# Attention states in 32-row tiles, and the output of four heads to a PSUM bank

## What is computed

```python
q = jax.nn.elu(q * E ** (-0.5)) + EPS_FEAT
k = jax.nn.elu(k) + EPS_FEAT
def step(carry, qkv_t):                       # one token after the other
    kv_s, k_s = carry
    q_t, k_t, v_t = qkv_t
    kv_s = kv_s + jnp.einsum('bhe,bhf->bhef', k_t, v_t)
    k_s = k_s + k_t
    num = jnp.einsum('bhe,bhef->bhf', q_t, kv_s)
    den = jnp.einsum('bhe,bhe->bh', q_t, k_s)[..., None] + EPS_DEN
    return ((kv_s, k_s), num / den)
...
return out @ W_out + b_out
```

## Time and profile before

| | us |
|---|---|
| median of 3 runs | 613.49 |
| lowest and highest | 611.41 to 614.47 |
| profiled execution, time | 610.65 |
| its span, first to last instruction | 608.9 |
| TensorE busy | 444.8 |
| VectorE busy | 345.6 |
| ScalarE busy | 237.6 |
| GpSimd busy | 331.3 |
| attention stage, about | 236 to 387 |

### The profile page before, as it was taken

One profiled execution on the slowest core, in us unless ns is written; L12 is line 12 of the kernel. 1 busy time (PEld: TensorE's weight loads), 2 busy tenths in 40 slices (PEclk: granted clock), 3 DMA queues, 4 the chain that ended last, 5 costly groups with the idle time before them and its releaser, 6 DMA issues.

```text
span 608.9 us, 12872 instructions
## 1 busy us (share of the span) xinstructions
PE 444.8 (73%) x4788; PEld 297.6 (49%) x4788; DVE 345.6 (57%) x984; ACT 237.6 (39%) x629; POOL 331.3 (54%) x259
## 2 busy tenths in 40 slices
PE   1884966997699325899999979149867599857970
PEld 1742543553345213677777768148335355433440
DVE  6396971221115992687777865485999222212097
ACT  4971212332224277555555530187611133322420
POOL 6184776888786601222222220004987788887691
PEclk9987875555569657799999986656978555555995
DMA  8998600101009980001111110541000000100592
GB/s 267 375 250 323 232 9 9 9 5 10 7 5 377 408 317 0 2 3 39 36 34 35 34 36 10 156 177 57 2 0 9 8 8 6 10 6 6 174 409 107
DMA packets 34389, 60.40 MB, mean 99 GB/s; under 512 B 12611, under 2 KB 18846, under 8 KB 33870
## 3 DMA queue, kind: packets, MB, share of 16 engines
q1 hardware_dynamic: 23078, 58.41, 26.8%
q0 software_dynamic: 11264, 1.38, 2.6%
HBM read 37.43 MB, written 29.36 MB: 110 GB/s over the span
## 4 chain that ended last, share of the span: by engine, by line
DVE 29%; PE 29%; issue 15%; DMA 13%; ACT 7%; POOL 5%; SPq 1%; POOLq 0%; DVEq 0%; another core or an unknown queue 0%; ACTq 0%
DVE X L973 9%; DMA rows_d<-A 5%; PE bank L897 5%; PE bank L778 4%; PE bank L878 4%; PE bank L795 3%; POOL planes_d L438 3%; DVE Cb L1075 3%; ACT A L508 3%; DMA planes_d<-Bb,put_i 2%; POOL A L452 2%; DVE bn L978 2%; DMA Bb<-planes_d 2%; PE bank L768 2%; PE bank L788 2%
## 5 line engine op out<-in xcount | busy, mean ns | idle before, releaser
L438 POOL DMA_INDIRECT planes_d<-Bb,put_i x64 | 100.4, 1569 | 24.6 <-issue 18.4
L452 POOL DMA_INDIRECT A<-rows_d,tok_i x64 | 71.9, 1124 | 20.6 <-issue 16.6
L1105 DVE TENSOR_TENSOR ring<-ring,bank 128x88 f32<-128x88 f32 x64 | 15.7, 246 | 103.7 <-ACT ring L576 72.0
L675 PE MATMUL bank<-ident,A 128*128 128x128 f32 x96 | 22.5, 412 | 55.1 <-ACT A L508 40.9
L479 POOL TENSOR_TENSOR Bb<-Cb,chm 128x576 f32<-128x576 f32 x16 | 19.0, 1220 | 66.8 <-DVE Cb L1139 33.4
L768 PE MATMUL bank<-ident,A 128*128 128x128 f32 x64 | 30.0, 469 | 29.3 <-DMA A<-rows_d,tok_i 23.2
L396 POOL TENSOR_TENSOR Bb<-Eb,st 128x512 f32<-128x512 f32 x8 | 8.9, 1112 | 74.7 <-DVE st L1023 74.7
L570 ACT ACTIVATE ring<-bank 128x128 f32<-128x128 f32 x64 | 17.7, 277 | 81.4 <-PE bank L768 70.7
L675 PEld LDWEIGHTS bank<-ident,A 128*128 128x128 f32 x96 | 18.2, 220 | 58.1 <-issue 29.9
L479 POOL TENSOR_TENSOR Bb<-w3s,chm 128x576 f32<-128x576 f32 x16 | 17.8, 1147 | 49.8 <-PE bank L920 49.8
L795 PE MATMUL bank<-w2s,ring 88*64 88x128 f32 x256 | 43.9, 446 | 0.0
(11 more groups left out here) (155 smaller groups left out, 1121.6 us busy)
## 6 DMA issues: line engine op xcount, KB each, us to landing
planes_d<-zeros SPq DMA_DIRECT2D x8, 2048.0 KB, 20.6
w3s<-in_w3T SPq DMA_DIRECT2D x2, 2816.0 KB
rows_d<-A SPq DMA_DIRECT2D x8, 512.0 KB, 11.5
A<-planes_d SPq DMA_DIRECT2D x8, 512.0 KB, 9.2
PL<-planes_d SPq DMA_DIRECT2D x8, 512.0 KB, 10.1
Cb<-planes_d SPq DMA_DIRECT2D x8, 512.0 KB, 10.8
Bb<-planes_d SPq DMA_DIRECT2D x8, 512.0 KB, 12.0
w1s<-in_w1T SPq DMA_DIRECT2D x1, 2816.0 KB
```

The costliest lines, as they stand in the source:

```text
L438: pool.indirect_dma_start(out=planes_d[f], in_=Y[:, s, :], in_offset=None, out_offset=bass.IndirectOffsetOnAxis(ap=put_i[:, s:s + 1], axis=0),
L452: pool.indirect_dma_start(out=A[:, t, :], out_offset=None, in_=rows_d, in_offset=bass.IndirectOffsetOnAxis(ap=tok_i[:, t:t + 1], axis=0), ...
L675: ins = pe.transpose(bank[g % 2][:, (i % 4) * P:(i % 4 + 1) * P], A[:, i, :], ident[:, :])
```

## The change

States. For each block q and chunk c, the 128x144 matmul becomes four of 128x32 rows and columns in the array: group j takes rows 32j to 32j + 31 of K's features (four heads) and the GW = 36 columns of those four heads, and its output goes to partitions 32j to 32j + 31 of one bank. A block's four chunks fit one bank (144 columns), so there are four batches (one per q) for eight, and `AFTER` is changed to suit. VectorE's mask is now `hm`, which says for each partition which of the four heads of its group it belongs to. SW holds 36 columns for each state where it held 144.

Output. The output goes to four banks, four heads each. The matmuls on the states take 32 partitions of QT and of SW, and 36 columns: 60 for 30. The four upper banks become one tensor, `upper`, so that the division runs once over all four banks.

Loop. TensorE's steps 1 to 6 are written out; the other engines keep their loops. The waits of the four engines that count `kv_ps` and `kv_sb` count four per step where they counted eight.

```diff
-    AFTER = ((), (0, 1, 2), (3, 4), (5, 6, 7))
+    AFTER = ((), (0, 1), (2,), (3,))
...
-        bank = [ctx.enter_context(nc.psum_tensor(f"bank{k}", [P, 512], F32)) for k in range(8)]
+        bank = [ctx.enter_context(nc.psum_tensor(f"bank{k}", [P, 512], F32)) for k in range(4)]
+        upper = ctx.enter_context(nc.psum_tensor("upper", [P, 4, 512], F32))
+        bank += [upper[:, k, :] for k in range(4)]
...
-                    for m in AFTER[g]:
-                        q = m // 2
-                        if m >= len(STATES):
-                            pe.wait_ge(kv_sb, PRIMED + NH * b + m + 1 - len(STATES))
-                        for k in range(1 if m == NH - 1 else 2):
-                            ins = pe.matmul(bank[STATES[m % len(STATES)]][:, k * VW:(k + 1) * VW], KN[:, 2 * (m % 2) + k, q, :],
-                                            VN[par][:, q, :, :].rearrange("p h f -> p (h f)"), start=True, stop=True)
+                    for q in AFTER[g]:
+                        if q >= len(STATES):
+                            pe.wait_ge(kv_sb, PRIMED + NQ * b + q + 1 - len(STATES))
+                        for c in range(NC if q < NQ - 1 else NC - 1):
+                            for j in range(4):
+                                ins = pe.matmul(bank[STATES[q % len(STATES)]][32 * j:32 * j + 32, c * GW:(c + 1) * GW],
+                                                KN[:, c, q, 32 * j:32 * j + 32],
+                                                VN[par][:, q, 4 * j:4 * j + 4, :].rearrange("p h f -> p (h f)"),
+                                                start=True, stop=True)
...
-                    ob = bank[4 + h // 8][:, 0:NC * HV].rearrange("p (c h f) -> p c h f", c=NC, h=8)
+                    ob = bank[4 + h // 4][:, 0:NC * GW].rearrange("p (c h f) -> p c h f", c=NC, h=4)
...
-                            before_c = SW[:, q, c - 1, :] if c else SW[:, q - 1, NC - 1, :]
-                            ins = pe.matmul(bank[4 + half][32 * q:32 * q + 32, c * HV:(c + 1) * HV], QT[par][:, t0:t0 + CHUNK],
-                                            before_c[:, half * HV:(half + 1) * HV], start=False, stop=True, skip_group_check=True)
+                            before_c = SW[rows, q, c - 1, :] if c else SW[rows, q - 1, NC - 1, :]
+                            o = c * GW
+                            ins = pe.matmul(bank[4 + g][32 * q:32 * q + 32, o:o + GW], QT[par][rows, t0:t0 + CHUNK],
+                                            before_c, start=False, stop=True, skip_group_check=True)
...
-            with pe.Fori(0, (B - 2) // 2) as i:
-                step(2 * i + 1, 1)
-                step(2 * i + 2, 0)
-            step(B - 1, 1, last=True)
+            for b in range(1, B):
+                step(b, b % 2, last=b == B - 1)
...
-                        dve.tensor_tensor(SW[:, q, 2 * (m % 2):2 * (m % 2) + n, :],
-                                          bank[STATES[m % len(STATES)]][:, 0:n * VW].rearrange("p (c v) -> p c v", c=n),
-                                          own[:, :].unsqueeze(1).broadcast_to([P, n, VW]), ALU.mult).then_inc(kv_sb, 1)
+                        dve.tensor_tensor(SW[:, q, 0:n, :].rearrange("p c (j f) -> p c j f", j=4),
+                                          bank[STATES[q % len(STATES)]][:, 0:n * GW].rearrange("p (c j f) -> p c j f", c=n, j=4),
+                                          hm[:, :].unsqueeze(1).unsqueeze(3).broadcast_to([P, n, 4, E + 1]),
+                                          ALU.mult).then_inc(kv_sb, 1)
...
-                for k in range(2):
...
+                dve.tensor_scalar(den.rearrange("p (g n) -> p g n", g=4), ob[:, :, :, E], DEN_EPS, None, ALU.add).then_inc(o_step, 1)
+                dve.wait_ge(o_step, 2 * b + 1)
+                dve.reciprocal(rec, den).then_inc(o_step, 1)
+                dve.wait_ge(o_step, 2 * b + 2)
+                dve.tensor_tensor(AN[:, :, :].rearrange("p c (g h f) -> p g c h f", g=4, h=4),
+                                  upper[:, :, 0:NC * GW].rearrange("p g (c h f) -> p g c h f", c=NC, h=4)[:, :, :, :, 0:E],
+                                  rec.rearrange("p (g c h) -> p g c h", g=4, c=NC).unsqueeze(4)
+                                  .broadcast_to([P, 4, NC, 4, E]), ALU.mult).then_inc(an_ready, 1)
```

More of the change, by code:

```diff
@@ L54, in macaron_kernel @@
     HV = VW // 2
+    GW = 4 * (E + 1)
     NQ = L // P
@@ L165, in macaron_kernel @@
         HTB, KT, QT0 = (Bb[:, o + k * L:o + (k + 1) * L] for k in range(3))
-        SW = Cb[:, 0:NQ * NC * VW].rearrange("p (q c v) -> p q c v", q=NQ, c=NC)
+        SW = Cb[:, 0:NQ * NC * GW].rearrange("p (q c v) -> p q c v", q=NQ, c=NC)
         VN0 = Cb[:, o:o + NQ * VW]
@@ L626, in copy_kn @@
                 act.wait_ge(kn_ps, b + 1)
-                act.wait_ge(kv_ps, PRIMED + NH * b)
+                act.wait_ge(kv_ps, PRIMED + NQ * b)
                 for c in range(NC):
@@ L828, in project @@
                 if not (isinstance(b, int) and b == 0):
-                    pe.wait_ge(kv_sb, PRIMED + NH * (b - 1))
+                    pe.wait_ge(kv_sb, PRIMED + NQ * (b - 1))
                     pe.wait_ge(q_read, 2 * b)
@@ L851, in turn_out @@
                     pe.wait_ge(kn_sb, PRIMED + NC * (b + 2))
-                pe.wait_ge(an_ready, 2 * (b + 1))
+                pe.wait_ge(an_ready, b + 1)
                 for c in range(NC):
@@ L905, in step @@
                 for h in range(HEADS):
-                    ob = bank[4 + h // 8][:, 0:NC * HV].rearrange("p (c h f) -> p c h f", c=NC, h=8)
+                    ob = bank[4 + h // 4][:, 0:NC * GW].rearrange("p (c h f) -> p c h f", c=NC, h=4)
                     for q in range(NQ):
                         o = (h // 4) * L + q * P + (h % 4) * CHUNK
-                        pe.matmul(ob[32 * q:32 * q + 32, :, h % 8, :], PR[:, o:o + CHUNK],
-                                  VX[:, q, h, :, :], start=(h % 8 == 0), stop=False, skip_group_check=True)
-                pe.wait_ge(kv_sb, PRIMED + NH * (b + 1))
+                        pe.matmul(ob[32 * q:32 * q + 32, :, h % 4, :], PR[:, o:o + CHUNK],
+                                  VX[:, q, h, :, :], start=(h % 4 == 0), stop=False, skip_group_check=True)
+                pe.wait_ge(kv_sb, PRIMED + NQ * (b + 1))
                 pe.wait_ge(sb_ready, (NQ - 1) * (b + 1))
-                for half in range(2):
+                for g in range(4):
+                    rows = slice(32 * g, 32 * g + 32)
                     for c in range(NC):
@@ L1137, in value @@
                     dve.wait_ge(vx_ready, PRIMED + NC * (b - 1))
-                    dve.wait_ge(kv_ps, PRIMED + NH * (b - 1))
+                    dve.wait_ge(kv_ps, PRIMED + NQ * (b - 1))
                 dve.tensor_tensor(VN[par][:, :, :, 0:E],
@@ L1170, in step @@
                                       ALU.mult).then_inc(sc_sb, 1)
[L1171 to L1174, removed]
-                        dve.tensor_tensor(SW[:, q, 2 * (m % 2):2 * (m % 2) + n, :],
-                                          bank[STATES[m % len(STATES)]][:, 0:n * VW].rearrange("p (c v) -> p c v", c=n),
-                                          own[:, :].unsqueeze(1).broadcast_to([P, n, VW]), ALU.mult).then_inc(kv_sb, 1)
-                        if q and m % 2:
-                            n = NC if q < NQ - 1 else NC - 1
-                            dve.wait_ge(kv_sb, PRIMED + NH * b + 2 * q + 2)
+                    for q in AFTER[g]:
+                        n = NC if q < NQ - 1 else NC - 1
+                        dve.wait_ge(kv_ps, PRIMED + NQ * b + q + 1)
+                        dve.tensor_tensor(SW[:, q, 0:n, :].rearrange("p c (j f) -> p c j f", j=4),
+                                          bank[STATES[q % len(STATES)]][:, 0:n * GW].rearrange("p (c j f) -> p c j f", c=n, j=4),
+                                          hm[:, :].unsqueeze(1).unsqueeze(3).broadcast_to([P, n, 4, E + 1]),
+                                          ALU.mult).then_inc(kv_sb, 1)
+                        if q:
+                            dve.wait_ge(kv_sb, PRIMED + NQ * b + q + 1)
                             if q > 1:
@@ L1192, in step @@
                     dve.wait_ge(anT_ps, PRIMED + b)
[L1193 to L1204 removed]
+                ob = upper[:, :, 0:NC * GW].rearrange("p g (n f) -> p g n f", f=E + 1)
+                den = top8[:, 0:8, :].rearrange("p a b -> p (a b)")
+                rec = top8[:, 8:16, :].rearrange("p a b -> p (a b)")
+                dve.tensor_scalar(den.rearrange("p (g n) -> p g n", g=4), ob[:, :, :, E], DEN_EPS, None, ALU.add).then_inc(o_step, 1)
[6 more added lines that the diff above has]
+                                  .broadcast_to([P, 4, NC, 4, E]), ALU.mult).then_inc(an_ready, 1)
             value(0, 0)
```

14 lines of the change are left out of this document (1 added, 13 removed).

## The result

The changed kernel takes 623.47 us (median; 622.70 to 625.01), the kernel before 612.45 beside it: a ratio of 1.018 [1.014, 1.022]. The prediction, 592.5 with a range of 583.5 to 604, was wrong, in sign too. The profiled execution has a span of 621.9 us for 608.9. In what follows each group of runs has the kernel before timed anew beside it, so ratios compare across groups and times don't; the ratios are of runs in the chip's faster state, which leaves out one run of e5.

What follows compares the result with a forecast made beforehand. TensorE was taken to bound the half-step from first state matmul to turn of K, 10.19 us becoming 7.57. Savings of 15.7 (steps 1 to 6), 1.8 (step 0) and 2.2 (last) total 19.7: forecast 592.5 us, range 583.5 to 604.

Steps and rivals of the forecast that it cites:

- The unrolled loop of TensorE: TensorE's attention steps written out: costed at nothing, since the straight-line first step's L920 takes the looped one's 1.20 us.
- State matmuls: TensorE, 60 of 128x32 at 0.0194 us each plus shape changes: 1.76 us a step for 4.14, 2.4 less.
- Matmuls on the states: TensorE, 30 become 60 of 32x32 with 36 columns: 1.36 us, plus 0.2 for shape change; 0.43 dearer per step.
- Rival (b): 32x32 matmuls cost what score matmuls do, 0.05 us each: 603 to 605 us; chance 0.12.
- VectorE: First state matmul to turn of K: VectorE needs 6.9 us, 0.6 ahead of TensorE; dear end 8.9.
- Rival (c): VectorE takes over that half at 8.9 us, leaving less gain: 601 us; chance 0.05.
- Division: VectorE's two rounds, some 2.0 us, become one of 1.6, reciprocal 0.6; saves 0.4 us once, at the stage's end.
- Period: Turn of K to turn of K in steps 1 to 6: 13.2 us; wrong if above 14 or clock 0.50 between.
- Last step: Last attention step, L909 and L920 assumed at half clock: 2.2 us gained.
- (a): Rival: the last step keeps its clock, gaining 7.6 us more: 585 us; chance 0.15.
- Rival (d): Fixed price of 25 ns per small-tile instruction, each group of 60 taking 3.0 us: about 618 us; chance 0.03.
- Rival (e): Narrow tiles make the clock fall inside the loop, 10.7 us per cold step: three give 623 us; chance 0.04.

Runs made afterwards that it cites:

- e5: Kernel before with only the output part (four banks, 60 narrow matmuls on the states, one division) and TensorE's steps written out: 623.11 us for 611.57, ratio 1.024.
- e2: Kernel before with TensorE's steps 1 to 6 written out and nothing else: 605.31 us for 605.65, ratio 0.999.
- e4: Changed kernel with TensorE's steps 1 to 6 as a loop of one step, GpSimd copying V and query feature to a fixed place: 604.16 us for 611.57, ratio 0.988.
- e7: Kernel before with TensorE's steps written out, plus 64 more 128x32 matmuls per step directly behind the in-chunk output: ratio 1.048.
- e6: Changed kernel with attention output stores and following loads moved behind the last step: pauses 13.9 us for 16.8 in one execution; time not compared.

## Why the prediction was wrong

**The step that failed** is "The unrolled loop of TensorE": "I cost this part at nothing". Its evidence was that step 0, straight-line, ran L920 in the same 1.20 us. That holds for the instructions of before, and e2 confirms it: 0.999. But the change was costed as if each part stood alone. It adds 150 matmul instructions to a step's 374 and 150 weight loads, and puts 248 of them behind each other in 2.4 us (188 before). Whether TensorE is supplied at that rate was asked nowhere. The runs show in its place that it is not: a packet, with some 127 matmul instructions and their loads, started every 3.3 us at best, and what was used up faster was waited for. The instruction queue stands on the page, 27 packets and 0.44 MB, and it was not read. With it the question would have been: without the loop all of the list is fetched, and where is it used up fastest? The size was 16.8 us of pauses, and some 14 that go with the clock.

**Point by point.**
- *State matmuls:* 1.76 forecast; 0.69, 0.40 and 0.33 in e4, 1.42. Right, a little dear: the 0.2 taken for each change of shape was too much, since 120 instructions at 9.8 ns are 1.18 and leave 0.24 for all three.
- *Matmuls on the states:* 1.36 forecast; 1.16 in e4 (310.20 to 311.36), changes of shape included; the in-chunk output 1.26 for 1.45. Rival (b), 0.05 each, falls: they cost what L909's do.
- *VectorE:* expected 0.6 ahead. In after it waits for the output (L1198) 32.9 us in all, and never holds up the turn of K in a full step. Rival (c) falls. But in e4 VectorE is the later one at L923, the 0.39 above: its first mask starts 0.93 behind the first state matmul (317.87 to 316.94), where the forecast had 0.1 ahead. The second operation of its query feature takes 1.52 there beside GpSimd's passes, for 0.69 in before; GpSimd's two copies, 1.2 us, move those passes there.
- *Division:* reciprocal 0.6 forecast, 0.553 measured; the last turn of the output waits 1.63 for 2.08, as forecast.

```profile
L1178 DVE TENSOR_TENSOR Cb<-bank,hm 128x144 f32<-128x144 f32 x24 | 6.6, 300 | 1.0 <-PE bank L899 1.0
...
L1186 DVE TENSOR_TENSOR Cb<-Cb 128x144 f32<-128x144 f32 x16 | 4.9, 309 | 1.1
...
L1200 DVE RECIPROCAL top<-top 128x64 f32<-128x64 f32 x8 | 4.4, 553 | 0.3
```

- *ScalarE's half:* 5.64 forecast unchanged, 5.58 in e4 (311.36 to 316.94).
- *Period:* 13.2 forecast; 12.98 in e4, but 20.2, 18.8, 19.1, 17.7, 16.5 and 15.5 in after. Both signs that the prediction named for being wrong came: periods over 14, and 0.50 between turns of K.
- *Last step:* states and in-chunk output at half clock as forecast (L913 2.15 for 1.31), the matmuls on the states at full, since the clock rises at 390. From the first scores to the turn of the output it is 15.8 us (377.14 to 392.96) for 20.4: a gain of 4.6, where 2.2 was forecast. (a) falls: the pause for ScalarE's copy (2.71) stays, and so does the half clock behind it.
- *Rival (d),* a fixed price of 25 ns per instruction: falls, 120 in 1.16 us are 9.7 ns each.
- *Rival (e),* the clock, had the right total (623) for a reason half right. The clock did fall in steps 1 to 6, but in e4 the same tiles keep 1.00 for five passes, so the tiles alone don't bring it down. In after it falls nine times up to 373 us, eight of them behind or in a pause of issue, down to one of 0.23; the first time, at 256.8, ahead of the first such pause and in a wait of 0.44 for VectorE. Behind the pause of 2.12 at 337.6 it doesn't fall. So pauses and narrow tiles together go with most of the falls, and no rule comes out of it. Stretches of after around the first fall, around a pause of 0.65 us at 294.0, and with the pause at 337.6 in it:

```profile
253.00:257.00 4.00, 3.56 (x184) 2.84 (x172) 3.93 (x11) 0.89 (x2) 0.00 (x0) 0.98 0.01 4
257.00:260.60 3.60, 1.86 (x107) 1.77 (x108) 1.37 (x4) 1.67 (x3) 0.00 (x0) 0.50 0.02 5
291.00:294.40 3.40, 3.01 (x155) 2.25 (x144) 3.23 (x9) 0.74 (x2) 0.00 (x0) 1.00 0.02 5
294.40:301.20 6.80, 6.54 (x225) 5.69 (x227) 2.93 (x7) 2.56 (x4) 0.00 (x0) 0.50 0.11 24
328.60:349.00 20.40, 17.75 (x735) 14.34 (x737) 13.60 (x29) 9.49 (x17) 4.46 (x4) 1.00 0.12 30
```

In before a pause of 0.60 stood in every step, with the clock at 1.00.

Still open: what starts a packet, and so which run is just dense enough. e2's runs of 188 matmul instructions in 2.4 us don't pause, e5's and e7's of 248 and 316 do.

## What to carry to other kernels

Count the instructions of a change, not only their time: a matmul cut in four has four times the instructions, and where they stand close, fetching them can be what TensorE waits for; the sign is "issue" as the releaser inside a group that has no wait, with an instruction packet that started 2.2 to 2.8 us before the pause ends. "Issue" alone is no sign: the feed-forward blocks have it too, with no packet near. A loop that is on hand runs them without a pause, so first ask how long its body becomes (here about 1,550 instructions stay, 1,800 don't), and rather halve the loop than write it out.

## What the runs showed of the hardware

- TensorE's instructions come in packets of 16.4 KB, in after never less than 3.29 us apart. In straight-line code a pause of 0.2 to 2.4 us stood at the end of a packet where narrow matmuls ran up to it, and ended 2.2 to 2.8 us behind the start of a packet (after, e5, e6, e7).
- Behind the taken branch of a loop too long to stay (1,800 and 2,150 instructions), TensorE stood for 4.1 to 4.7 us; behind that of one that stays (1,550), for 0.24 at most.
- Matmul instructions of 32x32 and 36 columns started 9.7 ns apart (e4), like those of 128x32.
- With pauses of up to 2.4 us the granted clock was 0.97 in e7 and 0.78 in after; with the tiles of after and no pause, 1.00 (e4, passes 2 to 6).
